# A decoder block on one core: transposes in two 64-row halves, and the first attention's output projection moved into its unit loop

## The reference

```
x = x + attn(layernorm(x))           # 16 heads of 64, causal softmax, output weights W_O
x = x + xattn(layernorm(x), ctx)     # 16 heads of 16, linear attention over a masked context
x = x + ffn(layernorm(x))            # 2 layers of:
    q, k, v = shift(y) @ wqkv        #   8 heads of 64; q and k normalised and rotated
    y += local_attention(q,k,v) @ wo #   windows of 128 tokens, each looks one window back
    y += (a * gelu(g)) @ w2 + b2     #   a, g = layernorm(shift(y)) @ w1 + b1
```

```
scores = einsum('bach,baCh->bacC', k, q)
attn   = softmax(where(causal, scores, -1e10) / sqrt(64))
z      = einsum('bacC,baCh->bach', attn, v)
out    = einsum('aeh,bach->bce', W_O, z)
```

## Time and profile before

| what | value |
|---|---|
| median of 3 runs | 1154.78 us |
| the profiled execution's own time | 1154.38 us |
| its span (first to last instruction) | 1152.6 us |
| PE busy | 1124.3 us (98%) |
| weight loads | 874.4 us (76%) |
| DVE / ACT / POOL busy | 790.9 / 691.6 / 610.0 us (69 / 60 / 53%) |
| chain that ended last | PE 90%, DVE 4%, POOL 2%, ACT 2%, issue 1%, DMA 0% |
| granted TensorE clock, mean | 0.996 of full speed |

### The profile page before, as it was taken

How to read it: one execution, slowest core, us unless ns; L and a number is a source line. 1 busy time by engine, 2 the same in 40 slices (tenths; PEclk the granted TensorE clock), 3 DMA queues, 4 the chain that set the end, 5 groups by cost and what they waited for, 6 DMA issues and landing times.

```text
span 1152.6 us, 20639 instructions
## 1 busy us (share of the span) xinstructions
PE 1124.3 (98%) x7114; PEld 874.4 (76%) x7114; DVE 790.9 (69%) x2417; ACT 691.6 (60%) x1712; POOL 610.0 (53%) x641
## 2 busy tenths in 40 slices
PE   8999999999999999999999999999999999999997
PEld 6777777777777766767667887877878878787676
DVE  6867677667767356778897677768667686675553
ACT  3668677777767224453676647657656566575832
POOL 1456666666664322049896446557465474573330
PEclk9999999999999999999999999999999999999999
DMA  7003333323210401030040001200002100001010
GB/s 255 1 2 132 100 109 113 123 93 123 89 71 2 164 19 55 1 112 22 19 176 1 2 1 36 94 1 1 1 19 99 55 1 1 1 32 42 19 38 18
DMA packets 30310, 64.72 MB, mean 56 GB/s; under 512 B 3840, under 2 KB 16256, under 8 KB 29696
## 3 DMA queue, kind: packets, MB, share of 16 engines
q1 hardware_dynamic: 30208, 63.41, 15.7%
HBM read 41.04 MB, written 22.36 MB: 55 GB/s over the span
## 4 chain that ended last, share of the span: by engine, by line
PE 90%; DVE 4%; POOL 2%; ACT 2%; issue 1%; DMA 0%; DVEq 0%; ACTq 0%; POOLq 0%
PE psum L1532 48%; PE psum L1633 7%; PE psum L1598 6%; PE psum L1615 6%; PE psum L1765 5%; PE psum L1814 5%; PE psum L1799 4%; PE psum L1781 4%; PE psum L1747 2%; PE psum L1827 1%; PE psum L1838 1%; PE psum L1721 1%; POOL rn L780 1%; PE psum L1829 0%; DVE y L1091 0%
## 5 line engine op out<-in xcount | busy, mean ns | idle before, releaser
L735 POOL TENSOR_TENSOR probs<-probs,rden 128x128 f32<-128x128 f32 (+3 forms) x256 | 177.6, 725 | 80.6 <-DVE rden L1149 80.6
L974 ACT ACTIVATE lp<-lp,lneg,rn 128x256 f32<-128x256 f32 (+1 forms) x256 | 143.6, 568 | 11.6 <-DVE lneg L1366 11.5
L890 ACT ACTIVATE probs<-probs,negmax 128x128 f32<-128x128 f32 (+3 forms) x256 | 139.9, 553 | 5.8 <-DVE negmax L1144 5.8
L1134 DVE CUSTOM_DVE_ANT_0 probs<-psum,causal 128x128 f32<-128x128 f32 (+3 forms) x256 | 110.3, 487 | 19.4 <-PE psum L1598 19.3
L768 POOL TENSOR_TENSOR lp<-lp,lrden 128x128 f32<-128x128 f32 x64 | 25.6, 400 | 165.8 <-DVE lrden L1371 165.8
L780 POOL TENSOR_TENSOR rn<-ssm,neg_half 128x8 f32<-128x8 f32 x64 | 108.4, 1693 | 0.0
L1354 DVE CUSTOM_DVE_ANT_0 lp<-psum,local 128x256 f32<-128x256 f32 (+1 forms) x256 | 84.2, 385 | 20.6 <-PE psum L1765 20.6
L771 POOL TENSOR_TENSOR lp<-lp,lrden 128x768 f32<-128x768 f32 x64 | 93.9, 1467 | 0.0
L1532 PE MATMUL psum<-wqkv_hi,hT_lo 128*128 128x512 f32 x192 | 82.0, 427 | 0.1
L961 ACT ACTIVATE sq<-psum 128x512 f32<-128x512 f32 x64 | 38.0, 594 | 68.9 <-PE psum L1532 68.9
L1633 PE MATMUL psum<-pT,v 128*64 128x256 f32 (+3 forms) x512 | 77.7, 446 | 1.4 <-DVE pT L1158 1.0
(11 more groups left out here) (172 smaller groups left out, 3146.7 us busy)
## 6 DMA issues: line engine op xcount, KB each, us to landing
w_raw<-in_w_all SPq DMA_DIRECT2D x22, 380.0 KB, 3.1
w_scratch<-w_half SPq DMA_DIRECT2D x22, 380.0 KB, 2.3
w_scratch<-w_rest SPq DMA_DIRECT2D x22, 380.0 KB, 3.0
x<-in_x SPq DMA_DIRECT2D x8, 512.0 KB, 7.4
aw<-in_w_quads SPq DMA_DIRECT2D x4, 768.0 KB, 5.5
wqkv_lo<-w_scratch SPq DMA_DIRECT2D x6, 512.0 KB, 6.3
wqkv_hi<-w_scratch SPq DMA_DIRECT2D x6, 512.0 KB, 4.5
w_hi<-w_scratch SPq DMA_DIRECT2D x2, 1364.0 KB, 6.5
```

The costliest lines, as they stand in the source:

```text
L735: ins = pool.tensor_tensor(pr, pr, rden[:, u % 2, h, i:i + 1].broadcast_to([P, TRI[i]]), ALU.mult)
L890: ins = act.activation(pr, pr, ACT.Exp, bias=negmax[:, u % 2, h, i:i + 1], scale=ADH ** -0.5, accum_out=den[:, u % 2, h, i:i + 1])
L974: ins = act.activation(pr, pr, ACT.Exp, bias=lneg[:, u % 2, h, w:w + 1], scale=rn[:, m % 2, w, 0, 2 * j + h:2 * j + h + 1], accum_out=lden ...
L1134: ins = dve.tensor_tensor_reduce(probs[:, u % 2, h, TRI_AT[i]:TRI_AT[i + 1]], bank[:, at:at + TRI[i]], causal[:, S - TRI[i]:S], 1.0, -3e38 ...
```

## The change

It has four parts.

1. Each transpose of a 128x128 block of `probs`, `lp` (local probabilities) and `ra` (rotated q and k) becomes two of 64 input rows: rows 0 to 63 against the upper left quarter of the identity, into one bank, rows 64 to 127 against the lower right quarter, into a second bank. Each gives 128x64. The bank of the first half is read by one engine, that of the second by the other, through strided destinations of 64 columns. `lqT` and `lkT` become one tile `lqkT`.
2. The 20 blocks of a unit are now three items of 8, 8 and 4 blocks (`T_BLOCKS`) in place of six.
3. The output projection is done for each quad and batch, when its two units are done: 16 items `awo.c.b` in place of four. It takes z and W_O as rounded halves: three products of 128x256 for each of two units and four token tiles. ACT rounds z out of PSUM (`zT_hi`), DVE subtracts (`zT_lo`), DVE adds each result to x (32 adds in place of 8). At the beginning ACT and POOL make the halves of W_O in four parts each. z moves from bank 4 to the banks 6 and 7, which the projections use and now the output projection too. `xnT_lo` no longer lies on x, and the second load of x is gone.
4. All order lists are written anew.

```diff
-T_BANKS = (4, 5, 2, 3, 4, 5)
-Z_BANK = 4
+T_BANKS = ((4, 5), (2, 3), (4, 5))
-T_TILES = ((0,), (1, 3), (2,))
+T_BLOCKS = (((0, 0), (0, 1), (0, 3)), ((1, 0), (1, 1), (1, 3)), ((0, 2), (1, 2)))
...
-        UNIT_PE = ("sA@2 z sB@2 pv@2 pk@3 pq@3 t0@1 t1@1 t2@1 t3@1 t4@1 t5@1")
+        UNIT_PE = ("t2@-2 sB z@-2 pk@1 pq@1 pv@1 t0@-1 t1@-1 awo@-2 sA@1")
-        UNIT_ACT = ("e0@1 e1@1 pv@2 aw2@2 pk@3 aw0@3 pq@3 aw1@3 t1@1 t3@1 part@1 t5@1")
+        UNIT_ACT = ("e0@-1 pq t1@-2 t3@-2 pv aw1 t5@-2 aw2 part@-2 e1@-1 z@-2 pk@1 aw0@1")
...
             wait_full(sp, plan["pv", NU - 1])
-            for b in range(B):
-                load_x(b)
...
+            def round_z(u):
+
+                c, j, b, pair = unit_at(u)
+                bank = wait_full(act, plan["z", u])
+                copy(zT_hi[:, b % 2, j % 2, :], bank[:, :]).then_inc(z_hi, 1)
...
-                dve.tensor_copy(zT[:, b, pair, :], bank[:, :]).then_inc(read[use[0]], 1)
+                dve.wait_ge(z_hi, u + 1)
+                dve.tensor_tensor(zT_lo[:, b % 2, j % 2, :], bank[:, :], zT_hi[:, b % 2, j % 2, :], ALU.subtract)\
+                    .then_inc(read[use[0]], 1)
...
+            def transposes(u, g):
+
+                pe.wait_ge(s_prob, 2 * u + (1 if g == 0 else 2))
+                uses = [plan["t", u, 2 * g + half] for half in range(2)]
+                banks_of = [wait_free(pe, use) for use in uses]
+                blocks = [(h, i, c) for h, c in T_BLOCKS[g] for i in range(c, T)]
+                for n, (h, i, c) in enumerate(blocks):
+                    lo = TRI_AT[i] + c * P
+                    for half in range(2):
+                        rows = slice(half * HP, (half + 1) * HP)
+                        ins = pe.transpose(banks_of[half][:, n * HP:(n + 1) * HP], probs[rows, u % 2, h, lo:lo + P],
+                                           ident[rows, rows])
+                        if n == len(blocks) - 1:
+                            ins.then_inc(full[uses[half][0]], 1)
...
-            def attention_output(b):
-                if b == 0:
-                    pe.wait_ge(ld_wo, 16)
-                wait_read(pe, plan["z", NU - QUNITS + 2 * b + 1])
+            def attention_output(c, b):
+                if c == 0 and b == 0:
+                    pe.wait_ge(wo_rest, 4)
+                wait_read(pe, plan["z", c * QUNITS + 2 * b + 1])
                 for tp in range(2):
-                    use = plan["awo", b, tp]
+                    use = plan["awo", c, b, tp]
                     bank = wait_free(pe, use)
                     for i in range(2):
                         t = 2 * tp + i
+                        rows = slice(t * P, (t + 1) * P)
                         ins = product(bank[:, i * D:(i + 1) * D],
-                                      [(zT[:, b, k, t * P:(t + 1) * P], woT[:, k, :]) for k in range(PAIRS)])
+                                      [(z[:, b % 2, k, rows], w[:, 2 * c + k, :]) for k in range(2)
+                                       for z, w in ((zT_lo, woT_hi), (zT_hi, woT_lo), (zT_hi, woT_hi))])
```

229 lines of the change are left out of this document (127 added, 102 removed), and 69 rows, old and new, of tables (CLOSE_DVE, ENTRY_ACT, ENTRY_DVE, ENTRY_PE).

## The result

The changed kernel takes 1159.34 us (median of four runs, 1158.94 to 1159.85), the kernel before 1153.97 in the same session (1151.73 to 1154.82). The ratio is 1.005, 95% interval 1.0032 to 1.0067: about 5 us slower, where 47 us faster was forecast and 1142 was the upper end of the range. The profiled execution has a span of 1157.3 us.

The account below looks back on a forecast made before the run. PE was taken to bound the kernel. From 1154.4 us: transposes -63, output projection -10, shape changes +8, unit-loop bank waits +6, last unit's softmax +3, passage waits +9, together -47, giving 1107 us; range 1078 to 1142.

Parts of the forecast that it names:

- The premise: Whole kernel: every microsecond taken from PE's stream shortens the kernel by one, as long as the others keep up.
- The price of a pair: All 1344 transposes: two halves cost 0.062 us in place of 0.109 for a block, saving 63 us.
- the slow rival: All transposes: a pair of halves costs as much as the block, 0.109 to 0.112 us; 1174 us, chance 9%.
- The changes of shape: PE's array-shape changes rise from 282 to 323, in the local layers; 41 at 0.19 us, +8 us.
- place 1 of "What becomes late": Unit loop: banks 6 and 7 serve z, projections and awo in turn; waits of 0.2 us a unit, 6 us.
- Readers of PSUM bind the unit loop: Unit loop: PE waits for banks 6 and 7, 1.1 us a unit, 35 us in place of 6; 1136 us, 17%.
- The output projection: PE's work for it falls from 55.7 to 45.3 us, saving 10 us.
- the passage: 400 to 600 us: three of four awo blocks (42 us) leave; 9 us of waits taken, bounds 0 and 20.
- Local layers and end: A local step gets 4.1 us shorter and 1.0 longer, without waits; stretches: -22 us local, -4 us end.
- the signs named: New profile: PE busy about 1062 us, 20 blocks 1.1 to 1.4, units 11.5 to 11.9; wrong if idle exceeds 60.

Follow-up runs that it names:

- e1: The kernel before with its own orders, only the transposes of the first attention halved: 1152.41 us, ratio 0.9992.
- e11: The kernel before with one of eight pairs in the output projection (32 in place of 256 instructions), adds kept: 1144.65 us, ratio 0.9931.
- e12: The changed kernel with old local orders and one of six products for each piece of the output projection (64 in place of 384 instructions): 1133.59 us, ratio 0.9831.
- e8: The changed kernel with plain f32 output projection, z and W_O not rounded, z read by DVE alone: 1166.07 us, ratio 1.0125.
- e3: The kernel before with its own orders and output projection, transposes halved in the first attention and the local layers: 1148.76 us, ratio 0.9955.
- e7: The changed kernel with the old orders for everything behind the last query projection (local layers and end), halves kept: 1148.23 us, ratio 0.9965.
- e2: The kernel before with its own orders, only the transposes of q, k and local probabilities halved: 1149.51 us, ratio 0.9969.
- e10: e1 with the copies out of the first attention's transpose banks cut to a quarter of the columns from unit 2 on: 1138.99 us, ratio 0.988.
- e13: e3 with q's projection in the unit loop moved between the second and third transpose items, DVE's and ACT's lists following: 1199.43 us, ratio 1.0403.

## Why the prediction was wrong, step by step

**The premise failed.** "So every microsecond taken out of PE's stream is a microsecond of the kernel, as long as the others keep up": PE was busy 98%, and I read that as PE being the bound in every stretch. e1 (27 us of PE, 0 to 1 us of time), e11 (48 us, 8) and e12 (38 us, 15) refute it. A list written out by hand fits PE's work into the latencies of the others; PE is then full and each chain just as long. "As long as the others keep up" I tested with average busy shares (DVE 71%, ACT 75%), and these say nothing of a copy of 0.69 us that stands between two items.

**The price of a pair** was right: 0.062 to 0.063 us within a run, against 0.062; the late second pair of a run makes it 0.066 to 0.071 on average, and 1344 x (0.109 - 0.069) = 54 in place of 63 us. The loads of the two halves do run beside each other, and the slow rival is out. With it goes what the Trainium skill's "TensorE: Matmul & The Clock Gate", section "LDWEIGHTS (loading the stationary operand)", would give, an estimate of 107 ns for a load of 128 columns.

**The changes of shape** cost nearly what was taken (0.19 us). Into the transposes the first pair is 0.09 us late and the second 0.05 (210.49 to 210.70 us in the loop); out of them the first product is 0.09 late and the second 0.10 (to 212.59 and 212.82). The mistake was to add them up over the kernel, +8, and not to set them against each block. For a block of seven between full-height products it comes to nothing, 1.24 against 1.23 us.

**Unit loop:** the term that failed is place 1 of "What becomes late", 0.2 us a unit for the banks 6 and 7. It measured 0.4: z's bank is read late, as said, and so is k's, which v's projection needs and which the prediction did not look at; by e8 k's chain alone is enough to hold the unit. Two slow units in every eight add 0.1 a unit. The rest is PE's work, which grew by 0.7 to 0.8 us a unit (transposes -0.9, output projection +1.5, changes of shape), where 0.5 was forecast. The rival *Readers of PSUM bind the unit loop* was right in kind; at 1136 us, with 1.1 us of waits a unit and no loss elsewhere, it took too much here and nothing in the local layers.

**The output projection** was costed at 10 us saved, and at the passage becoming some 42 us shorter without it. The passage did (-39.3 us from z.29 to hT.0, forecast about -40, with waits of its own: PE is idle 15 of 92 us there, at a clock of 0.96). That is no contradiction to e11, where the adds to x stayed in the passage and PE waited 19.5 us for them; here 28 of the 32 adds went with the products. But what the passage gave, the loop took: 14 projections of 3.05 us are 43 us there, where 40 was forecast. The move brought nothing (e3 and e7 agree within their intervals).

**Local layers and end:** here most of the error lies, 35 of 51 us. "I take no waits there", a step 3 us shorter. It is as long as before. PE's starts come 2.8 us closer at a step's transposes, not 4.1; 1.3 us of it goes at the changes of shape and 2.1 us is now idle time. The halves with the old lists give 0.9 us a step (e2, e7); the new lists take it back, and 7 us more at the end, where PE is idle 11% of 1000 to 1100 us and the clock falls to 0.95.

**Of the signs named,** busy PE near 1062 came out as 1093.7 (the late starts are counted as busy); 20 blocks in 1.1 to 1.4 us was right; units of 11.5 to 11.9 us are 12.6; the passage was right in length, but DVE was busy 71.3 of the 92.2 us from z.29 to hT.0, 77% and not above 85%; PE's idle time is 64 us, beyond the 60 at which I called the forecast wrong.

What stays open: what the unit loop would take with z or k in a bank of its own, what the new unit orders would bring with the projection left in the passage (neither was run), and which of the new local lists costs the 10 us; e7 changed all four engines and the end at once.

## What to carry to other kernels

A full engine in a hand-ordered program is not yet the bound: before a gain is counted at full price, follow in the timeline what reads the bank it fills and what its next item waits for, and ask of work that is moved what wait it was filling. When an instruction gets cheaper but changes the array's shape, hold the block with both its neighbours against the old one; here seven transposes between full-height products gained nothing, ahead of 64-row scores 0.3 us. And compare starts, not busy shares: PE was 99% busy in units that lost 0.4 us to late starts. The complete versions that beat the kernel before, e2 (1149.51 us), e3 (halves with the old orders, 1148.76) and e7 (1148.23), all keep the old local orders; the first two do it without touching the projection.

## What the runs showed of the hardware

- Two transposes of 64 rows by 64 columns of output, one in each half of the array, start 62 to 63 ns behind the two before them (e10, after), 66 to 71 on average over a run of 14 to 32 instructions, whose second pair starts 0.11 us behind the first; the whole block takes 109.
- Idle time in total does not tell the granted clock. e11's PE was idle 58.5 us, with waits of 10.3, 9.2 and 5.0 us, at a mean clock of 0.979, and at 0.54 to 0.78 in the three stretches of 10 us shown above. e13's was idle 96.3 us at a mean of 0.994; from 100 to 400 us, with two waits of about a microsecond in each unit, it was busy 253 of 300 us at 1.00.
